# Attention with experts on one core: q and k in two float16 parts, two heads in the halves of the array

## The reference

```
qkv = x @ W_qkv;  q, k = rope(q, k)                      # 16 heads, 16 dimensions
att = einsum('bhtd,bhsd->bhts', q, k) / 4 + causal mask
y   = softmax(att) @ v @ W_o;  x = layernorm(x + y)
gate = softmax(x @ Wg + bg), the two largest, scaled to sum 1
x = layernorm(x + sum over the two experts of gate * (We @ x + be))
```

## Time and profile before

| | |
|---|---|
| median of 3 runs (range) | 3236.32 us (3235.18 to 3238.13) |
| span of the profiled execution | 3236.3 us, the same as the median within 0.1 |
| PE busy | 3109.0 us, 96% |
| DVE busy | 2677.5 us, 83% |
| ACT busy | 1884.1 us, 58% |
| POOL busy | 1200.8 us, 37% |
| one of the 14 turns of MIDDLE | about 192 us |

### The profile page before, as it was taken

One profiled execution on the slowest core, in us unless ns is written; L12 is line 12 of the kernel. 1 busy time (PEld: TensorE's weight loads), 2 busy tenths in 40 slices (PEclk: granted clock), 3 DMA queues, 4 the chain that ended last, 5 costly groups with the idle time before them and its releaser, 6 DMA issues.

```text
span 3236.3 us, 58547 instructions
## 1 busy us (share of the span) xinstructions
PE 3109.0 (96%) x18752; PEld 1711.5 (53%) x18752; DVE 2677.5 (83%) x8452; ACT 1884.1 (58%) x4253; POOL 1200.8 (37%) x1414
## 2 busy tenths in 40 slices
PE   5789999999999999999999999999999999999987
PEld 2234555555555555555555555555555555555555
DVE  7687888888888888888888888888888888888745
ACT  2456556565655657556565655656565565755651
POOL 3253424343243443424344342434334244442110
PEclk8799999999999999999999999999999999999997
DMA  6344424433432433444233443433443243344000
GB/s 143 58 70 76 65 60 72 65 68 66 83 60 55 80 59 71 63 81 65 48 79 59 79 64 67 67 62 68 66 83 60 59 76 62 68 65 69 3 27 14
DMA packets 174819, 210.95 MB, mean 65 GB/s; under 512 B 26008, under 2 KB 124592, under 8 KB 174256
## 3 DMA queue, kind: packets, MB, share of 16 engines
q1 hardware_dynamic: 173056, 202.98, 36.1%
q10 hardware_dynamic: 1456, 4.23, 0.4%
HBM read 138.44 MB, written 67.11 MB: 64 GB/s over the span
## 4 chain that ended last, share of the span: by engine, by line
PE 84%; DVE 8%; issue 3%; ACT 2%; DMA 1%; POOL 1%; SPq 0%; ACTq 0%; DVEq 0%; POOLq 0%
PE bank L1052 23%; PE attend L1147 15%; PE scores L1125 14%; PE bank L1109 14%; PE bank L1089 6%; PE bank L1171 3%; PE bank L1098 3%; DVE bank L902 2%; PE bank L1155 1%; PE bank L1077 1%; PE bank L1162 1%; PE bank L1179 1%; DVE maxima L905 1%; PE bank L1203 1%; PE bank L1188 1%
## 5 line engine op out<-in xcount | busy, mean ns | idle before, releaser
L778 ACT ACTIVATE weights<-scores 128x512 f32<-128x512 f32 (+3 forms) x3072 | 1333.1, 494 | 926.0 <-PE scores L1125 913.5
L902 DVE CUSTOM_DVE_ANT_0 bank<-bank,far_q 128x128 f32<-128x128 f32 (+3 forms) x2048 | 962.9, 512 | 202.4 <-PE bank L1109 186.0
L1125 PE MATMUL scores<-q_stack,k_stack 99*128 99x512 bf16 (+3 forms) x3072 | 822.1, 329 | 16.6 <-DMA q_stack<-lowrows 7.3
L1109 PE MATMUL bank<-k_stack,q_stack 96*128 96x512 bf16 (+3 forms) x3072 | 799.5, 332 | 26.3 <-DMA k_stack<-parts_scratch 8.3
L692 POOL TENSOR_SCALAR_AFFINE_SELECT weights<-weights 128x512 f32<-128x512 f32 x512 | 325.5, 637 | 1253.5 <-ACT weights L778 1253.3
L905 DVE TENSOR_REDUCE maxima<-bank 128x1 f32<-128x512 f32 x1024 | 644.1, 682 | 72.6 <-PE bank L1109 72.4
L1147 PE MATMUL attend<-weights,values 128*32 128x512 f32 (+3 forms) x6144 | 583.0, 494 | 1.4 <-POOL weights L692 1.0
L1125 PEld LDWEIGHTS scores<-q_stack,k_stack 99*128 99x128 bf16 x3072 | 279.8, 97 | 417.8 <-ACT weights L778 151.6
L1109 PEld LDWEIGHTS bank<-k_stack,q_stack 96*128 96x128 bf16 x3072 | 276.7, 98 | 398.5 <-issue 166.4
L1052 PE MATMUL bank<-wexp_hi,zT_hi 128*128 128x512 f32 x1024 | 382.2, 454 | 11.1 <-DVE lowrows L922 11.1
L1026 DVE SCALAR_TENSOR_TENSOR z<-bank,picked,z 128x256 f32<-128x256 f32 x512 | 247.6, 484 | 114.6 <-PE bank L1052 105.6
(11 more groups left out here) (115 smaller groups left out, 3133.3 us busy)
## 6 DMA issues: line engine op xcount, KB each, us to landing
parts_scratch<-parts SPq DMA_DIRECT2D x128, 384.0 KB, 2.5
q_stack<-parts_scratch SPq DMA_DIRECT2D x384, 128.0 KB, 7.2
k_stack<-parts_scratch SPq DMA_DIRECT2D x384, 128.0 KB, 7.8
x_in<-in_x SPq DMA_DIRECT2D x64, 256.0 KB, 3.6
z<-in_x SPq DMA_DIRECT2D x32, 512.0 KB, 4.6
out<-z SPq DMA_DIRECT2D x32, 512.0 KB, 3.1
q_stack<-lowrows SPq DMA_DIRECT2D x192, 8.0 KB, 2.4
z<-in_w_exp ACTq DMA_DIRECT2D x1, 1024.0 KB, 5.1
```

The lines of the kernel that those rows point to most:

```text
L778: act.activation(weights[:, n % NW, hh, c0:CH], st[(QUAD * n + hh) % NS][:, c0:CH], ACT.Exp, scale=DH ** -0.5).then_inc(S["weights_ready"], 1)
L902: dve.tensor_tensor_reduce(out=b[:, 0:w], in0=b[:, 0:w], in1=far_q[:, CH - w:CH], scale=1.0, scalar=-SENTINEL, op0=ALU.add, op1=ALU.max, a ...
L1109: pe.matmul(b[:, 0:w], q_stack[0:ROWS, n, hh, qt * P:(qt + 1) * P], k_stack[0:ROWS, n, hh, kc * CH:kc * CH + w], start=True, stop=True).th ...
L1125: pe.matmul(st[(QUAD * n + hh) % NS][:, c0:CH], k_stack[0:MROWS, s, hh, kb * P:(kb + 1) * P], q_stack[0:MROWS, s, hh, qc * CH + c0:(qc + 1 ...
```

## The change

q and k are split into two float16 parts instead of three bfloat16 parts, and three products of parts (TERMS) replace six, so a head has 48 rows instead of 96, and 51 with the maxima. The rows of heads 0 and 2 of a group lie from partition 0, those of heads 1 and 3 from partition 64 (`pair`). A matmul of ST or B now names a tile of 64 rows by 128 columns, at row 0 or row 64. The split has one CAST step per half: one cast on ACT, one subtraction on GpSimd or VectorE. The maxima are written in three parts of fixed steps (MAX_STEPS), with the step sizes in `k_stack`; these rows come from a column that GpSimd fills (`max_step`) and that VectorE copies to both halves at the start. LOAD has 12 transfers as before, of 64 KB instead of 128; MT has six of 4 KB instead of three of 8. In the tables, ST and B come in pairs (h = 0, 1 and h = 2, 3) with nothing between the two; a word that stood inside a pair stands before or after it, and the second CAST words are gone. All else keeps its place.

```
-TERMS = ((0, 0), (0, 1), (1, 0), (1, 1), (0, 2), (2, 0))
+TERMS = ((0, 0), (0, 1), (1, 0))
+NPART = 2
 ROWS = len(TERMS) * DH
-MROWS = ROWS + 3
+MAX_STEPS = (2.0 ** 15, 2.0 ** 5, 1.0)
+MROWS = ROWS + len(MAX_STEPS)
+PAIRS = 2
+HALF_ROWS = P // PAIRS
...
-ST.16.0 ST.16.1 MOE.0.0.1 CAST.0.3.0 ST.16.2 B.1.3.1 B.1.3.2 MOE.0.0.2 B.1.3.3 ST.16.3 PV.14 PV.15 YE.1.0
+ST.16.0 ST.16.1 MOE.0.0.1 B.1.3.0 B.1.3.1 MOE.0.0.2 B.1.3.2 B.1.3.3 ST.16.2 ST.16.3 PV.14 PV.15 YE.1.0 CAST.0.3
...
+        def rest(eng, c, s, k):
+            eng.wait_ge(S["cast"], c.at("cast", ("CAST", s, k)))
+            eng.tensor_tensor(parts[:, k % 2, 1], half_of(c, s, k), parts[:, k % 2, 0], ALU.subtract) \
+               .then_inc(S["parts_ready"], 1)
+
+        def pair(stack, rows, n, hh, cols):
+            base = HALF_ROWS * (hh % PAIRS)
+            return stack[base:base + rows, n, hh // PAIRS, cols]
...
-                            src = scratch[which, parts_qk[which], QUAD * n:QUAD * (n + 1)]
-                            sp.dma_start(stack[DH * t:DH * (t + 1), n, :, :], src.rearrange("h d t -> d h t")) \
-                              .then_inc(S[f"stack{n}"], DMA)
+                            for i in range(PAIRS):
+                                src = scratch[which, parts_qk[which], QUAD * n + i:QUAD * (n + 1):PAIRS]
+                                row = HALF_ROWS * i + DH * t
+                                sp.dma_start(stack[row:row + DH, n, :, :], src.rearrange("h d t -> d h t")) \
+                                  .then_inc(S[f"stack{n}"], DMA)
...
-            dve.memset(k_stack[ROWS:MROWS, :, :, :], -1.0).then_inc(S["const_v"], 1)
             dve.wait_ge(S["const_p"], CONST_P)
+            for i in range(PAIRS):
+                rows = slice(HALF_ROWS * i + 32, HALF_ROWS * (i + 1))
+                last = k_stack[rows].rearrange("p s h t -> p (s h t)")
+                dve.tensor_copy(last, max_step[rows, 0:1].to_broadcast([32, SLOTS * QUAD // PAIRS * T])) \
+                   .then_inc(S["const_v"], 1)
...
-                    pe.matmul(b[:, 0:w], q_stack[0:ROWS, n, hh, qt * P:(qt + 1) * P],
-                              k_stack[0:ROWS, n, hh, kc * CH:kc * CH + w], start=True, stop=True).then_inc(fu, 1)
+                    pe.matmul(b[:, 0:w], pair(q_stack, ROWS, n, hh, slice(qt * P, (qt + 1) * P)),
+                              pair(k_stack, ROWS, n, hh, slice(kc * CH, kc * CH + w)), start=True, stop=True) \
+                        .then_inc(fu, 1)
...
-                    pe.matmul(st[(QUAD * n + hh) % NS][:, c0:CH], k_stack[0:MROWS, s, hh, kb * P:(kb + 1) * P],
-                              q_stack[0:MROWS, s, hh, qc * CH + c0:(qc + 1) * CH], start=True, stop=True) \
+                    pe.matmul(st[(QUAD * n + hh) % NS][:, c0:CH], pair(k_stack, MROWS, s, hh, slice(kb * P, (kb + 1) * P)),
+                              pair(q_stack, MROWS, s, hh, slice(qc * CH + c0, (qc + 1) * CH)), start=True, stop=True) \
```

More of the change, by code:

```diff
@@ L269 @@
-ST.40.0 ST.40.1 ST.40.2 MOE.1.2.3 ST.40.3 PV.38 PV.39 YE.3.0
+ST.39.0 ST.39.1 MOE.1.2.2 ST.39.2 ST.39.3 MASK.39
+ST.40.0 ST.40.1 MOE.1.2.3 ST.40.2 ST.40.3 PV.38 PV.39 YE.3.0
 ST.41.0 ST.41.1 ST.41.2 ST.41.3 MOE.1.3.0
@@ L370, in ledger @@
                 add(f"resid_loaded{step[1]}", seg, step)
-            if step[0] == "CAST" and not step[3]:
-                add("rest_ready", seg, step)
-            if step[0] == "CAST" and step[3]:
+            if step[0] == "CAST":
                 add("parts_ready", seg, step)
@@ L620, in work @@
                         half = ((0, 0, 1) if c.seg == "pre" else (None, 0, 0, 1))[s]
-                        waits = [(f"parts_stored{i}", c.at(f"parts_stored{i}", ("CAST", half, 2 + i, 1), DMA))
+                        waits = [(f"parts_stored{i}", c.at(f"parts_stored{i}", ("CAST", half, 2 + i), DMA))
                                  for i in range(2)]
@@ L636, in work @@
                     emptied(sp, c, step)
-                    for part in range(3):
-                        dst = q_stack[ROWS + part:ROWS + part + 1, n, :, :]
-                        sp.dma_start(dst.rearrange("o h (t q) -> o (h t) q", q=P), maxrow[:, part, :]) \
-                          .then_inc(S[f"maxrow{n}"], DMA)
+                    for part in range(len(MAX_STEPS)):
+                        for i in range(PAIRS):
+                            row = HALF_ROWS * i + ROWS + part
+                            dst = q_stack[row:row + 1, n, :, :]
+                            src = maxrow[i * QUAD * TILES // PAIRS:(i + 1) * QUAD * TILES // PAIRS, part, :]
+                            sp.dma_start(dst.rearrange("o h (t q) -> o (h t) q", q=P), src) \
+                              .then_inc(S[f"maxrow{n}"], DMA)
                 elif kind == "XR":
@@ L664, in _ @@
                                pattern=[[-1, P]], channel_multiplier=1).then_inc(S["const_p"], 1)
+            pool.memset(max_step[:, :], -MAX_STEPS[0]).then_inc(S["stepped"], 1)
+            for n, (row, size) in enumerate((HALF_ROWS * i + ROWS + part, MAX_STEPS[part]) for i in range(PAIRS)
+                                            for part in (1, 2)):
+                pool.wait_ge(S["stepped"], n + 1)
+                pool.affine_select(out=max_step[:, :], in_=max_step[:, :], compare_op=ALU.not_equal, fill=-size, base=-row,
+                                   pattern=[[1, 1]], channel_multiplier=1).then_inc(S["stepped"], 1)
+            pool.wait_ge(S["stepped"], 2 * PAIRS + 1)
             no_weight = pool.to_reg(0.0)
```

393 lines of the change are left out of this document (194 added, 199 removed).

## The result

The kernel after takes 3455.09 us (median of 4 runs, 3447.88 to 3465.95), the kernel before 3236.32: a ratio of 1.068, 95% interval 1.066 to 1.070. A fourth execution of the kernel before took 3981.93 us, far longer than the other three, and is left out. The prediction, 3209 with a range of 3070 to 3320, was wrong in sign and too low by 246 us. The profiled execution has a span of 3454.5.

The account below looks back on a forecast made before the run. PE's instruction stream was taken as the bound (96% busy). From 3236 us, middle turns gave -13, last table +2, first table -12, early table -1 and start -3: -27, so 3209 us, range 3070 to 3320.

Parts of the forecast that it names:

- (1): ST and B matmuls of a middle turn: two halves run together, the second costing about 7 ns; gain 29.9 us a turn.
- (3): Second ST of a pair waits for ACT's exponential one pair back, not three matmuls back: +17.0 us a middle turn.
- (4): B and other products wait for one of four banks; DVE has room but PE arrives sooner: +1.0 us a turn, 0 to 3.
- C: Rival for ST and B pairs: halves hinder each other, a pair lasting 1.3 times one matmul; 3308 us; chance 0.10.
- D: Rival for ST and B pairs: halves take turns, no gain, while switches and buffer waits stay; about 3490 us; chance 0.06.
- (2): PE's tiling changes between ST or B and full-array products: 100 more a middle turn at 0.11 us, +11.0 us.
- (5): One cast pass on ACT and subtraction on POOL fewer per half, off PE's path in a turn: 0.
- Last table and POST: Last table: pairs -22.5, switches +8.1, buffers +16, together +2 us, from -1 to +5; POST not touched.
- Start: Before the tables: first stack load about -5 us, maxima rows +1.8, memset replaced by copies; -3 in the sum, early table -1.
- First table: Pairs -26.2, switches +2.8, buffers +13.5, plus shorter casts and stack load: -12 us, from -4 to -20.
- A clock under 1.00: Sign that the forecast is wrong: PE's granted clock under 1.00 inside the middle turns, where it was 1.00 before.
- B: Rival at each pair's second ST: waits behind ACT's queued work make a turn 4 to 5 us longer; about 3290 us; chance 0.20.

## Why the prediction was wrong, step by step

(1) *Pairs: right.* -29.9 predicted, -30.5 by the account, which prices all 192 pairs as side by side. 130 of the 192 pairs of a turn start within 20 ns, nearly all of those within 4, and a pair of 512 columns follows a pair after 0.226 us in the median. The other 62 pairs are late, and their lateness is in the waits of (3) and (4). So rivals C and D fell, and the column quarters of the earlier trace rows were the right neighbour to read from. The Trainium skill's 3.07 times for four row tiles (TensorE: Matmul & The Clock Gate, Measured speedup vs the span model), read over to two halves as an estimate from that page, would make a pair 1.3 matmuls long; for two halves this trace shows 1.05 (0.226 against 0.216).

(2) *Switches: right.* +11.0 predicted, +10.1 measured, 0.09 to 0.10 for each border (MOE to B 0.33 where the stream is 0.23). The Trainium skill, TensorEngine Tiling (Array Packing), Key Properties, says that a change of tiling mode drains the engine; the holes in this trace agree.

(3) *Score buffers: right in size, for more than one reason.* +17.0 predicted, +16.4 measured. The full array in pairs already has 8.8, since a fourth ST in a row comes too soon at 0.216 us apart as well. The rest belongs to the speed of the pairs.

(4) *Banks: the step that failed.* +1.0 (0 to 3) predicted, +12.2 measured; the 11.2 us between are 157 in 14 turns, of the 246 us by which the total was missed. The step put nearly nothing on the banks because DVE has room, 165 of 192 us, and PE only "arrives sooner". That is an argument from load. The one I had just made for the score buffers, from the count of buffers and the distance of requests, holds for the banks word for word: two B take two banks at once, two pairs all four, and the next product waits for a reduction of 0.68 us begun a moment ago (9.7 us of the waits are on DVE), or for a projection's copy behind ACT's exponentials (4.7 us, on an engine that the step did not look at). Of the 12.2 us, 5.6 come with the order alone, in the full array, where no product is faster than before; 6.6 come with the halves. The run with three banks shows the sensitivity: one buffer less, 38 us a turn more. The Trainium skill, TensorEngine Tiling (Array Packing), PSUM Bottleneck, says that tiling speeds up TensorE but not the emptying of PSUM, a sentence that spoke against this change and that I did not weigh; the trace agrees with it in the 6.6 us, for the other 5.6 need no tiling. The remaining 3.5 us a turn of the account have no releaser that the trace names. And while this turn has a clock of 1.00 throughout, others have 0.98 or 0.99 in the mean and last 205 to 207 us, with PE's busy time up from 186 to as much as 190 us: some 2 us more a turn that go with the clock, which the prediction had at nothing.

(5) *Casts: right.* 0 to -0.9 predicted; 0.6 us less a turn in the full array and the order of before.

*Outside the turns.* Last table and POST: +2 predicted, +12.2 measured; about half of the difference is bank waits again, the other half has no releaser that the trace names. Start: -4 predicted, -7.7 measured. First table: -12 predicted, +24 measured; the pairs gave some 32 us there by the account, more than I reckoned, but its clock fell from 0.97 to 0.77. PE's busy time rose by 17 us, from 156.3 to 173.2, with less to do, and its idle time by 7; no run separates what the clock alone costs there. A clock under 1.00 was on my list of what would show the forecast wrong, for the turns; for the first table it had no term and no rival.

*The rivals.* The actual course is nearest to B, slower by waits, with the place wrong: B's lateness of ACT at the second ST is in the 16.4 us, and its bank part comes to 3 or 4 us by its own sum. No rival had the order of the words as its mechanism, though the order was the larger of the two things that the change does: the edit in pairs without halves is slower by 14.7 us a turn, and halves without the pairs are no slower in a turn. The change was costed against the order of before, by what its halves give; its two parts should each have been costed alone. (The low ends of the sum for a turn add up to -6.3 us, not -6.1; nothing hangs on it.)

## What to carry to other kernels

When a change makes an engine faster, or puts requests of one kind next to each other, count the buffers between the engine and its readers, and lay out when requests come, not how busy the readers are: three score buffers and four banks served a stream of singles at 96% busy, and cost 31 us a turn to a stream of pairs. Two products side by side should draw on different buffers and different readers (here one ST and one B), so that a pair asks no more of each than a single did. Where a change does two things, run each alone: a two by two of four kernels named the cause that no single trace did.

## What the runs showed of the hardware beyond that

Products of different kinds, row counts (51 and 48) and targets run side by side in the two halves, with starts at most 8 ns apart and 3 in the median.

In the first table the granted clock was 0.95 to 0.98 in all four kernels with ST and B in the full array (before, bfloat16 in pairs, and the two with zero rows), and 0.71 to 0.86 in the nine with halves (0.77 after, 0.78 with the order of before, 0.71 in one run with the same first table as after). In the same order, full array against halves, this is 176.4 against 201.0 us, and 184.3 against 203.0. So the fall comes with the halves and not with the order; which property of theirs does it, and why it differs among runs of one table, stays open. Before two of its falls in the kernel after, at 181.6 and 198.7 us, PE was busy 8.0 and 8.5 of 10 us at a clock of 1.00; in the kernel before, PE was busy 7.5 of 10 us (200 to 210 us) and the clock stayed at 1.00. In middle turns, with full-array MOE products between, the clock stays at 0.98 to 1.00 except where PE waits most (0.94 with three banks).
